# Products that nobody reads, in the tails of two attentions and ahead of the first routed tile

## What is computed

```python
# layer 0: attention over x (B, D=256, T=512), 8 heads, masked rows and columns, queries = keys = values
q = xt @ Wq.T
logits = (scores * cmask + (1.0 - cmask) * NEG) * rmask
ctx = einsum(softmax(logits), qh);  out = (ctx @ Wo.T).transpose
# layer 0: eight experts, two for each token
probs = softmax(x @ w_router);  topk_w, topk_i = top_k(probs, 2)
for ex in range(8):
    hid = silu(x @ w_gate[ex]) * (x @ w_up[ex])
    out = out + coef[:, ex] * (hid @ w_down[ex])
# layer 1: attention with 16 heads, RMS norms, scale and shift from the condition, o + o @ W_out
# layer 1: a dense gated block with low-rank corrections for eight experts
x = x + L0_ffn(L0_attention(x, cond))
x = x + L1_ffn(L1_attention(x, cond))
```

## Time and profile before

| | us |
|---|---|
| median of 3 runs | 2002.25 (2002.22 to 2002.59) |
| the profiled execution | 1989.18 |
| its span, first to last instruction | 1987.50 |
| TensorE busy | 1654.1 (83% of the span) |
| VectorE busy | 1083.0 (54%) |
| first attention, up to its last logits | 0 to 523.6 |
| first routed tile starts | 568.5 |
| last scatter-add of the routed stage is issued | 841.5 |
| second attention ends on VectorE | 1396.1 |

### The profile page before, as it was taken

One profiled execution on the slowest core, in us unless ns is written; L12 is line 12 of the kernel. 1 busy time (PEld: TensorE's weight loads), 2 busy tenths in 40 slices (PEclk: granted clock), 3 DMA queues, 4 the chain that ended last, 5 costly groups with the idle time before them and its releaser, 6 DMA issues. The chain is left out here.

```text
span 1987.5 us, 31522 instructions
## 1 busy us (share of the span) xinstructions
PE 1654.1 (83%) x10250; PEld 959.7 (48%) x10250; DVE 1083.0 (54%) x2020; ACT 581.2 (29%) x1096; POOL 275.9 (14%) x343
## 2 busy tenths in 40 slices
PE   5788888888248899755778888887899999999998
PEld 1132333232124455442344444444777777777776
DVE  4455656553555445325355655563566666666665
ACT  0333433444323223123344334342111121121121
POOL 4211111011542123211111101110000000000000
PEclk7899999999579999955798989988899999999999
DMA  5422211111597999461111101110850000000000
GB/s 161 146 60 60 59 43 41 34 43 51 182 296 140 203 197 245 76 216 32 32 44 44 37 17 32 44 43 23 139 109 1 11 11 0 11 11 0 11 11 11
DMA packets 195488, 145.43 MB, mean 73 GB/s; under 512 B 126492, under 2 KB 163120, under 8 KB 195336
## 3 DMA queue, kind: packets, MB, share of 16 engines
q1 hardware_dynamic: 179000, 109.84, 21.7%
q0 software_dynamic: 15632, 34.30, 8.0%
q10 hardware_dynamic: 768, 0.13, 0.0%
HBM read 50.95 MB, written 41.56 MB: 47 GB/s over the span
## 5 line engine op out<-in xcount | busy, mean ns | idle before, releaser
L1866 PE MATMUL d_bank<-XTh,d_wgu 128*128 (+1 forms) x1408 | 244.7, 273 | 0.0
L1953 ACT ACTIVATE d_SG<-d_bank 128x256 f32<-128x256 f32 x264 | 101.4, 384 | 381.6 <-PE d_bank L1866 301.8
L329 DVE TENSOR_REDUCE W<-a_bn 128x1 f32<-128x512 f32 x256 | 163.5, 686 | 85.5 <-PE a_bn L243 82.1
L2015 DVE SCALAR_TENSOR_TENSOR d_HF<-d_bank,d_SG 128x256 f32<-128x256 f32 x264 | 112.2, 425 | 171.0 <-ACT d_SG L1953 152.7
L1866 PE MATMUL d_bank<-XTl,d_wgu 128*128 (+1 forms) x704 | 192.4, 273 | 0.0
L311 ACT ACTIVATE W<-a_bt 128x512 f32<-128x512 f32 x256 | 144.1, 596 | 152.9 <-PE a_bt L262 151.9
L1866 PEld LDWEIGHTS d_bank<-XTh,d_wgu 128*128 128x128 f16 x1408 | 138.2, 98 | 18.0
L280 PE MATMUL a_bc<-W 128*64 128x512 f32 x512 | 142.7, 637 | 0.0
L243 PE MATMUL a_bn<-W 97*128 97x512 f16 x256 | 99.8, 422 | 48.1 <-DVE W L329 28.5
L1113 PE MATMUL b_G<-W,R 128*128 x468 | 79.7, 322 | 53.2 <-issue 53.2
L2022 DVE TENSOR_TENSOR d_H_l<-d_HF,d_H_h 128x256 f16<-128x256 f32 x264 | 112.4, 426 | 9.0
(11 more groups left out here) (286 smaller groups left out, 3050.8 us busy)
## 6 DMA issues: line engine op xcount, KB each, us to landing
W<-W SPq DMA_DIRECT2D x96, 64.0 KB, 3.0
W<-W POOLq DMA_DIRECT2D x96, 64.0 KB, 2.6
W<-in_x SPq DMA_DIRECT2D x8, 512.0 KB, 3.8
W<-W SPq DMA_DIRECT2D x32, 128.0 KB
x<-x_rows SPq DMA_DIRECT2D x8, 512.0 KB, 11.7
c_a_A<-c_H SPq DMA_DIRECT2D x64, 64.0 KB, 3.1
c_a_B<-c_H POOLq DMA_DIRECT2D x64, 64.0 KB, 2.8
c_a_CT<-c_a_CS SPq DMA_DIRECT2D x32, 128.0 KB
```

The costliest lines, as they stand in the source:

```text
L329: self.nc.vector.tensor_reduce(self.NM[:, s * cols:(s + 1) * cols], self.bn[s % 2][:, :].rearrange("p (k n) -> p k n", k=cols), AX, ALU.ma ...
L1866: mm = MM(b[:, w * CH:(w + 1) * CH], wgu[:, f, w, KF * s + k, :], X[m][:, k, toks], start=(w == 0 and k == 0 and i == 0), stop=(k == KF - ...
L1953: nc.scalar.activation(SG[k % 3][:, :], GU[(f + 3) % 4][:, 0:CH], ACT.Silu, scale=1.0 / WS).then_inc(silu, 1)
L2015: V.scalar_tensor_tensor(out=HF[:, :], in0=b[:, CH:2 * CH], scalar=1.0 / WS, in1=SG[k % 3][:, :], op0=ALU.mult, op1=ALU.mult).then_inc(mul ...
```

## The change

TensorE gets three groups of products whose results nobody reads. No wait, signal or transfer is added or moved.

- A new step `hold` at the head of the tail of each attention. Only TensorE's tables have it. In both it is twenty products of 128x512 float16 into `bn[1]`: in layer 0 of the identity with a row tile of `g.R`, in layer 1 of normed activations with the query weights.
- In `layer0_routed`, behind the waits for `tabled` and `hidden_clear` and ahead of the tile loop, 280 products of 128x128 float16, `ones` with `tri`, into the bank `O[0]`, whose first use is `down(0)`.

```diff
 def walk(plan, table, b=None, b1=None, b2=None, last=None):
-    batch = {"first": b, "slot": b, "route": b, "rank": b, "place": b, "nat": b1, ...}
+    batch = {"first": b, "slot": b, "route": b, "rank": b, "place": b, "hold": last, "nat": b1, ...}
@@ batches
-    walk([("recip",), ("spread",), ("rows",), ("out",), ("logit",)], steps, last=end)
+    walk([("hold",), ("recip",), ("spread",), ("rows",), ("out",), ("logit",)], steps, last=end)
@@ layer0_attention, TensorE
+                def hold(n):
+                    row = g.R[:, 0, HEAD:ROW].bitcast(F16)[:, 0:T0]
+                    for _ in range(20):
+                        nc.tensor.matmul(a.bn[1][:, :], g.identh[:, :], row, start=True, stop=True)
@@ layer0_routed, TensorE
                 pe.wait_ge(tabled, 1)
                 pe.wait_ge(hidden_clear, 4)
+                for _ in range(280):
+                    MM(O[0][:, 0:P], r.ones[:, :], r.tri[:, :], start=True, stop=True)
                 tile = None
                 for i in range(MT):
@@ layer1_attention, TensorE
+                def hold(n):
+                    for _ in range(20):
+                        nc.tensor.matmul(a.bn[1][:, :], XNh[0][:, 0, 0:P], wqh[:, 0, 0:T0], start=True, stop=True)
```

More of the change, by code:

```diff
@@ L136, in walk @@
 def walk(plan, table, b=None, b1=None, b2=None, last=None):
-    batch = {"first": b, "slot": b, "route": b, "rank": b, "place": b, "nat": b1, "shift": b1, "recip": last, "spread": last, "out": last, "rows": last, "logit": last}
+    batch = {"first": b, "slot": b, "route": b, "rank": b, "place": b, "hold": last, "nat": b1, "shift": b1, "recip": last, "spread": last, "out": last, "rows": last, "logit": last}
     for name, *args in plan:
@@ L609, in table @@
                     return {"first": lambda n: a.pe_first(pe, n), "slot": lambda n, s: a.pe_slot(pe, n, s),
-                            "rank": rank, "nat": nat, "shift": lambda n: a.pe_shift(pe, n, uses),
+                            "rank": rank, "hold": hold, "nat": nat, "shift": lambda n: a.pe_shift(pe, n, uses),
                             "q0": lambda n: q_tile(n, uses, 0), "q1": lambda n: q_tile(n, uses, 1),
@@ L1470, in table @@
                     steps = {"first": lambda n: a.pe_first(pe, n), "slot": lambda n, s: a.pe_slot(pe, n, s),
-                             "nat": lambda n, s: a.pe_nat(pe, n, s), "shift": lambda n: a.pe_shift(pe, n, uses),
+                             "hold": hold, "nat": lambda n, s: a.pe_nat(pe, n, s), "shift": lambda n: a.pe_shift(pe, n, uses),
                              "xt0": lambda n: x_turned(n, uses, 0), "xt1": lambda n: after_x(n, uses),
```

## The result

The median went from 1997.47 us (1992.78 to 2003.23) to 2008.23 us (2000.47 to 2014.53), over 22 executions of each kernel on the same chip. The ratio is 1.0050, 95% interval 1.0038 to 1.0062, which is 7.6 to 12.4 us; the means differ by 9.8 us. The sign was right and the forecast of 2017.0 was 8.8 us too high. The three times that were shown of before (median 2002.25) lay high in its own spread.

The account below looks back on a forecast made before the run. TensorE, busy 83% of the span, was seen waiting at the routed stage's opening and in both tails. 1989.18 profiled, +17.1 - 1.3 + 0 - 1.0 gave 2003.98; with 13.07 carried over, 2017.0 us, 8-in-10 range 2008.5 to 2021.

Parts of the forecast that it names:

- That the 280 products lie behind the wait, not in it: Routed stage's opening: TensorE's 37 us idle ends at 567.48, the products begin there, so they delay the first tile.
- Their price: The 280 products: 35 at 0.107 us, then 245 at 0.057, 17.6 us in all; first tile 17.1 us late.
- Tile 0 warm, -1.3: First routed tile: 5.06 us before, 3.75 at the high clock after the products, so -1.3 us.
- Nothing absorbs the delay: Routed stage behind tile 0: all is chained to that tile, nothing taken off, stage ends 15.8 us later.
- Taken at 0, bound -2.9: Low-clock stretch at 656.7 to 663.3 us: may not fall there in the new alignment; 0 taken, at best -2.9 us.
- First tail 0: First attention's tail: 6.2 us idle remain, the clock falls again, credit 0; bound -3.75 us.
- Second tail -1.0: Second attention's tail: 3.1 us idle remain; -2.6 us if the clock stays up, 0 if it falls; -1.0 taken.
- The offset of 13.07: Whole kernel: timed median 2002.25 lay 13.07 us above the profiled execution, unexplained by the trace, carried over unchanged.
- (a): Rival: clock stays high in both tails and at 656 us, +6.55 us, 2008.8; chance 0.09.
- (b): Rival: the 280 products run slow, +28.4 us (2030.6) if all at 0.107, or 2024 if 175 are; chance 0.09 together.
- (c): Rival: without the profiler tile 0's rows land late enough to hide the 280 products, -7.7 us, 1994.6; chance 0.07.
- (d): Rival: routed stage absorbs 12 or more of the 15.8 us, no effect that can be told, 2002 to 2006; chance 0.05.

Follow-up runs that it names:

- e1: The changed kernel without the twenty products in each tail, the 280 kept; 2011.26 us against 2000.52 for the kernel before, ratio 1.0051.
- e4: The changed kernel with the 280 products doubled to 560; 2018.16 us against 2000.52 for the kernel before, ratio 1.0081.
- e7: The kernel before with 27 awaited scratch clears on GpSimd ahead of the clears TensorE waits for; 2013.55 us against 1999.21, ratio 1.0083.
- e6: The changed kernel once more, unchanged, for a second profiled execution; 1999.75 us.
- e11: The changed kernel with 44 and 32 tail products, and 16 8-column and 124 512-column products ahead of the clears' wait replacing the 280; 1998.93 us against 1998.26, 1.0002.
- e5: The kernel before once more, unchanged, for a second profiled execution; 1994.71 us.
- e2: The changed kernel without the 280 products, the twenty in each tail kept; 1998.08 us against 2000.52 for the kernel before, ratio 0.9991.
- e8: The changed kernel with 124 products of 512 columns ahead of the clears' wait instead of the 280 behind it; 1994.08 us against 1999.21, ratio 0.9981.
- e3: The changed kernel with 480 128-column products ahead of the clears' wait instead of the 280 behind it; 2011.83 us against 2000.52, ratio 1.0052.
- e12: The kernel before with 48 8-column and 124 512-column products ahead of the clears' wait, none in the tails; 1992.83 us against 1997.46, ratio 0.9980.

## Why the prediction was right and wrong

What failed is one term and the baseline. The later routed stage was taken at 0 and gave back 5.0 us, for a reason that the prediction did not have; and the sum was laid on a median of three executions that stood 4.8 us over that of 22. The serial cost of the filler, the main term, was right.

**That the 280 products lie behind the wait, not in it: right.** They began at the clears' end, with the idle 36.35 us ahead of them.

**Their price: right.** 17.6 us forecast, 18.44 in the profile above, 17.52 in e1. The 0.45 us for fetching the expert's number did not come on top: the first product of tile 0 follows the last filler product directly. The delay was forecast as 17.1 and is 16.7 in the averages. The sum by 81 ns for each product, as the Trainium skill, TensorE: Matmul & The Clock Gate, section Back-to-back issue gap, has it, would have been 22.7 us; the 56 ns that e4 shows decide against it here.

**Tile 0 warm, -1.3: right, and sized too small.** 3.27 us became 1.96 for its first group. The whole tile took 3.75 us warm, as priced, but the 5.06 of before was the shortest of four executions without the filler (5.06 to 6.68): the gain is 2.1 us in the mean. That tiles 0 to 11 took just 1.3 us less in the averages is partly chance.

**Nothing absorbs the delay: right,** shown by e7: 15.7 us in, 15.1 out, with the stage as long as ever. The timed executions of e4 (19.0 us for 26) stay unexplained.

**"Taken at 0, bound -2.9": wrong, and the term that decides.** I had seen the low stretch behind tile 11 and said that it might not fall in the new alignment. The stretch went away in all three profiles with the filler (after, e6, e1), and with it the stall ahead of it or most of it: -5.0 us, not 0, and not -2.9. Two things were mis-sized. I counted only the half of the low stretch's busy time; the stall that brought it on (2.90 us of idle in TensorE) is a cost of its own and goes with it. And I took it as a matter of luck in time, while it was tied to where in the order of TensorE's instructions their fetch falls, which the change moves in a fixed way. 600 added instructions are also 600 instructions to be fetched, and I gave them no other price than their run time.

**First tail 0: right.** The clock fell again in the 6.08 us that were left. **Second tail -1.0: wrong by that much.** The spread was 0.47 us shorter, and nothing of it arrived at the logits. (Its bound on the bad side is 0.9 us by the prediction's own numbers, 1373.3 + 8.5 against 1380.92, and not 1.2; it played no part.) The rule of the Trainium skill, the same page, section Why this matters for your kernels, to keep gaps short, did what it says to the clock in the gap (1.00 through 3.0 us); e11, with 0.58 us of gap, shows that even a fully warm spread brings no time here, since TensorE isn't what the tail waits for.

**The offset of 13.07: wrong in kind.** I carried the difference between the profiled execution and the median over as if it were a property of the kernel. Over 22 executions the median of before is 1997.47, so 8.3 of the 13.07 us were the luck of that one profiled execution (its second attention took 531.4 us against 536.4 in e5 and 539.8 in e2, its tiles 0 to 11 79.3 against 81.7 and 83.5; its first attention was not short, 493.5 against 489.3 and 489.4), and the other 4.8 that of three timed ones. From 1997.47 my own sum would have given 2012.3; with -5.0 for the two steps and 0 for the second tail, 2008.3, and 2008.23 was measured. So of the 8.8 us by which the forecast was high, 4.8 are the baseline and 4.0 the terms.

**The rivals.** (a), the clock high wherever it may, has the nearest time, 2008.8, for other reasons: of its three places one stayed high, and it was carried by the same offset. (b) fell with the pace of 0.056. (c), that the rows of tile 0 come later in other executions, fell with e1, e4 and e7. (d), that the stage absorbs 12 us or more of the delay, fell with e7, though the stage did get shorter.

## What to carry to other kernels

Work given to an idle engine is free only ahead of the wait that ends the idleness: the same idea behind the wait costs its full length (+16.7 us), ahead of it none, and even there it should be few wide instructions and not many narrow ones (e8 against e3). Before a change of time is put down to what an edit does, compare a version that adds the same number of instructions and hardly any work, since their mere count can move a stall. And take the baseline from many executions: a profile is one of them, and here its distance to the median was luck.

## What the runs showed of the hardware that I had not expected

- The fetch of instructions shares the DMA engines with the data. One packet of 16 KB on a load of 704 KB makes one of the load's 16 signals come at 7.4 to 8.6 us, with the other 15 there by 6.4, and the load 1 to 2 us late for its reader (waits of 3.5 to 4.7 us in the seven profiles with a packet on the load, 2.2 to 2.5 in the seven without). In six of the seven the clock fell behind that stall too, 4.2 to 5.2 us in all (18.5 to 19.3 for the two steps against 14.1 to 14.3).
- 48 products of 8 columns, 1.7 us of work in idle time, made the kernel 0.54% faster (0.9946 [0.9929, 0.9964], six executions); 128 of them changed nothing (1.0001 [0.9982, 1.0019]).
- A stream of 128-column products fell into gaps after 289 of them, behind a stretch with the DMA engines full (27 products in 12 us, gaps up to 1.8 us), where 124 products of 512 columns ran through for 29 us. No instruction packet ended the gaps; their cause is open.
- One program's clock differs between its executions in both attentions: 58.0 and 61.4 us of low time up to the same product in two executions of before, 47.8 and 54.6 in two of after. In the second attention 180.4 and 187.6, 191.0 and 180.5 us of low time went with 531.4 and 536.4, 539.9 and 531.8 us.
- VectorE waited 15.41 us for an operation that takes 0.69 us, only in the version with 44 products in the first tail (2.16 us ahead of it in e12). It was not found why.
